# Layer 3's expert MLP in a 13-stage graph network: tokens as the stationary operand, slots on the partitions

## What is computed

```
router_probs = softmax(xf @ router_w);  expert_index = argmax;  expert_gate = max
position_in_expert = cumsum(mask) * mask;  mask *= position < C
expert_inputs  = einsum("td,tec->ecd", xf, dispatch)              # (8, 64, 768)
h              = gelu(einsum("ecd,edm->ecm", expert_inputs, w1) + b1)   # (8, 64, 192)
expert_outputs = gelu(einsum("ecm,emd->ecd", h, w2) + b2)         # (8, 64, 768)
out            = einsum("ecd,tec->td", expert_outputs, combine);  x = x + out
```

## Time and profile before

| | |
|---|---|
| median of 3 runs | 3299.75 us (3291.88, 3299.75, 3300.95) |
| the profiled execution | 3296.41 us, span of its instructions 3294.6 us |
| PE busy | 3065.6 us, 93% |
| DVE, ACT, POOL busy | 52%, 23%, 43% |
| the chain that ended last | PE 85%, DVE 9%, issue 3%, ACT 2% |

### The profile page before, as it was taken

The page is one execution under the profiler, slowest core; times in us unless marked ns, Lnnn a source line. Parts: engine busy times, 40 slices in busy tenths (PEclk is TensorE's granted clock), DMA queues, the critical chain, the costliest instruction groups (busy, mean ns, idle before and its releaser), DMA issues.

```text
span 3294.6 us, 38724 instructions
## 1 busy us (share of the span) xinstructions
PE 3065.6 (93%) x13979; PEld 2397.6 (73%) x13979; DVE 1713.4 (52%) x2808; ACT 754.8 (23%) x1333; POOL 1427.1 (43%) x1007
## 2 busy tenths in 40 slices
PE   8999899999999987898997989899999998989978
PEld 3577577888888884676776468578888886778858
DVE  7734699474556435636765546433344436641141
ACT  1043211232333212102244122211111103121222
POOL 2022287524544360563440045366666664536600
PEclk9999899899999998998998999999999999999987
DMA  2011266212222121222210232133333322213313
GB/s 82 15 48 44 91 192 222 70 43 68 75 72 66 58 82 40 87 86 64 66 58 10 71 112 72 45 93 99 96 95 95 95 86 67 72 48 100 96 32 132
DMA packets 92132, 259.35 MB, mean 79 GB/s; under 512 B 10431, under 2 KB 11071, under 8 KB 91716
## 3 DMA queue, kind: packets, MB, share of 16 engines
q1 hardware_dynamic: 80352, 219.45, 21.8%
q10 hardware_dynamic: 11652, 38.19, 3.5%
HBM read 256.03 MB, written 1.57 MB: 78 GB/s over the span
## 4 chain that ended last, share of the span: by engine, by line
PE 85%; DVE 9%; issue 3%; ACT 2%; DMA 0%; ACTq 0%; DVEq 0%
PE ps L429 22%; PE ps L433 22%; PE ps L434 22%; DVE aux L2004 3%; PE ps L909 2%; PE ps L537 1%; PE ps L531 1%; PE ps L1269 1%; PE ps L995 1%; PE ps L801 1%; PE ps L790 1%; PE ps L783 1%; PE ps L775 1%; DVE hot L2454 1%; DVE row L1814 1%
## 5 line engine op out<-in xcount | busy, mean ns | idle before, releaser
L367 POOL TENSOR_SCALAR w_hi<-raw 128x768 fp32r<-128x768 f32 x498 | 461.9, 928 | 1654.6 <-PE ps L429 1445.6
L370 POOL TENSOR_TENSOR w_lo<-raw,w_hi 128x768 fp32r<-128x768 f32 x498 | 973.6, 1955 | 41.5
L429 PE MATMUL ps<-H_hi,w_hi 128*128 128x512 f32 x804 | 319.9, 398 | 21.1 <-issue 11.6
L429 PE MATMUL ps<-A_hi,w_hi 128*128 128x512 f32 x780 | 309.2, 396 | 12.1 <-ACT scr L1594 12.1
L433 PE MATMUL ps<-H_lo,w_hi 128*128 128x512 f32 x804 | 316.6, 394 | 0.0
L434 PE MATMUL ps<-H_hi,w_lo 128*128 128x512 f32 x804 | 316.5, 394 | 0.0
L429 PE MATMUL ps<-B_hi,w_hi 128*128 128x512 f32 x720 | 292.2, 406 | 21.3 <-DVE B_lo L1798 15.2
L433 PE MATMUL ps<-A_lo,w_hi 128*128 128x512 f32 x780 | 305.7, 392 | 0.0
L434 PE MATMUL ps<-A_hi,w_lo 128*128 128x512 f32 x780 | 305.2, 391 | 0.0
L433 PE MATMUL ps<-B_lo,w_hi 128*128 128x512 f32 x720 | 283.3, 393 | 0.0
L434 PE MATMUL ps<-B_hi,w_lo 128*128 128x512 f32 x720 | 283.1, 393 | 0.0
(11 more groups left out here) (490 smaller groups left out, 5802.1 us busy)
## 6 DMA issues: line engine op xcount, KB each, us to landing
raw<-stream_dram SPq DMA_DIRECT2D x558, 384.0 KB, 3.1
w_ring<-w_dram ACTq DMA_DIRECT2D x45, 384.0 KB, 3.6
u_rows<-rows_dram ACTq DMA_DIRECT2D x8, 768.0 KB, 5.8
rows<-rows_dram ACTq DMA_DIRECT2D x7, 768.0 KB, 4.0
w_last<-w_dram ACTq DMA_DIRECT2D x9, 384.0 KB, 3.6
x<-x_dram ACTq DMA_DIRECT2D x1, 1536.0 KB, 9.4
out_dram<-x ACTq DMA_DIRECT2D x1, 1536.0 KB, 5.1
orf<-orf_dram ACTq DMA_DIRECT2D x6, 192.0 KB, 3.0
```

The costliest lines, as they stand in the source:

```text
L367: pool.tensor_scalar(w_hi[:, b // 3, b % 3], raw[:, b // 3, b % 3], 1.0, 1.0, ALU.mult, ALU.mult)\
L370: pool.tensor_tensor(w_lo[:, b // 3, b % 3], raw[:, b // 3, b % 3], w_hi[:, b // 3, b % 3], ALU.subtract)\
L429: mm = pe.matmul(o, wh, xh, start=first, stop=False, skip_group_check=True)
```

## The change

Only ffn3 and its data change. In step 1 DVE makes all four comparisons without a wait between, then all four casts, each with a signal of its own (PE waits for them tile by tile in the first bank), then the bias selector `row` (8 x 512) and the four scalings. The up product is turned round: 64 slots of one expert are stationary, the 192 unpadded hidden columns move; experts 2m and 2m+1 write to partitions 0 to 63 and 64 to 127 of bank m. DVE copies the bank to scr, PE turns it by two transposes of 128x96 (`slots_turned`), ACT adds b1 and makes the gelu as before on 96 partitions. The down product has 64 slots (96 rows of hidden) stationary and w2's rows move, 384 columns at a time; b2 comes by a matmul of 8 rows in front of each bank. ACT makes the gelu in PSUM and the high part, DVE the low part; the results lie with slots on the partitions, so `to_nodes(scr)` and the split after it go. The transposes of the scaled one-hots move between the down tiles (`weights_turned`, banks 6 and 7). The stream holds 28 used blocks and 2 of zeros in place of 36; ACT issues one more small DMA (slot_b, 8 x 768) behind that of tri. b2 leaves the column table (48 columns fewer in the first load).

```diff
-TURNS = dict(..., mlp3=8, ffn3=6)
+TURNS = dict(..., mlp3=8, ffn3=5)
...
+                            if j == 0 and h == 0:
+                                pe.wait_ge(dve_to_pe, S.due(dve_to_pe))
                             mm = pe.matmul(ps[:, j], bn[:, m, j * P:j * P + P], e_hi[:, m], ...
...
-                for n in range(3):
-                    for f in range(KC):
...
-                                mm = pe.matmul(ps[:, f, c], raw[:, f // 3, f % 3, k], acc[:, k, c], start=k == 0,
...
-                                mm = pe.matmul(ps[:, f, e * 64:e * 64 + 64], raw[:, f // 3, f % 3, k],
-                                               hidden[:, q // 8, q % 8 * 64:q % 8 * 64 + 64], start=h == 0, stop=h == 1,
...
-                to_nodes(scr)
+                def slots_up(m):
+                    use(m)
+                    for c in range(3):
+                        i = 3 * m + c
+                        whole_block(turn + i // 6, i % 6)
+                        for q in range(4):
+                            e, k = (4 * c + q) // KC, (4 * c + q) % KC
+                            if m == 0 and e == 0:
+                                pe.wait_ge(act_to_pe, S.due(act_to_pe))
+                            mm = pe.matmul(ps[64 * e:64 * e + 64, m, 0:FF], acc[:, k, m * P + 64 * e:m * P + 64 * e + 64],
+                                           raw_at(i % 6)[:, q * FF:q * FF + FF], start=k == 0, stop=k == KC - 1,
...
+                        whole_block_used()
+                    done(mm, m, "dve")
+
+                def slots_turned(m):
+                    b = 4 + m % 2
+                    use(m)
+                    use(b)
+                    for h in range(2):
+                        mm = pe.transpose(ps[0:96, b, h * P:h * P + P], scr[:, m, h * 96:h * 96 + 96], ident[:, :])
...
+                    done(mm, b, "act")
+
+                def slots_down(m):
+                    banks = ((0, 1), (2, 3), (4, 5), (0, 1))[m]
+                    pe.wait_ge(act_to_pe, S.due(act_to_pe))
+                    for g in range(2):
+                        use(banks[g])
+                        mm = pe.matmul(ps[:, banks[g], 0:384], row[0:8, m * P:m * P + P],
+                                       w1_ring[0:8, 0, g * 384:g * 384 + 384], start=True, stop=False, skip_group_check=True)
...
+                    for q in range(4):
+                        e, h = q // 2, q % 2
...
+                        for g in range(2):
+                            mm = pe.matmul(ps[64 * e:64 * e + 64, banks[g], 0:384],
+                                           hidden[0:96, m, h * P + 64 * e:h * P + 64 * e + 64],
+                                           raw_at(i % 6)[0:96, g * 384:g * 384 + 384], start=False, stop=h == 1,
...
+                slots_up(0)
+                for m in range(1, NT):
+                    slots_up(m)
+                    slots_turned(m - 1)
+                pe.wait_ge(dve_to_pe, S.due(dve_to_pe))
+                slots_down(0)
+                slots_turned(NT - 1)
+                for m in range(1, NT):
+                    if m < 3:
+                        weights_turned(2 * m - 2)
+                        weights_turned(2 * m - 1)
+                    slots_down(m)
+                for b in range(4, 6):
+                    whole_block(turn + 4, b)
+                unpend()
                 graph_t("dve")
...
+                def slots_out(m):      # ACT
+                    banks = ((0, 1), (2, 3), (4, 5), (0, 1))[m]
+                    for g in range(2):
                         act.wait_ge(tile_for["act"], S.due(tile_for["act"]))
+                        S.step(act.activation(ps[:, banks[g], 0:384], ps[:, banks[g], 0:384], ACT.Gelu_apprx_tanh))
+                        act.copy(bn[:, m, 384 * g:384 * g + 384], ps[:, banks[g], 0:384]).then_inc(act_to_dve, 1)
...
-                    S.step(dve.tensor_copy(e_hi[:, m], aux[:, m]))
+                    dve.tensor_copy(e_hi[:, m], aux[:, m]).then_inc(dve_to_pe, 1)
+                S.step(dve.tensor_copy(row[0:8, :].rearrange("p (e c) -> p e c", e=8), ...
+                for m in range(NT):
                     S.step(dve.tensor_scalar(aux[:, m], aux[:, m], nv[:, 12, m:m + 1], None, ALU.mult))
                 mark(dve_to_pe)
```

More of the change, by code:

```diff
@@ L409, in whole_block, with raw_at @@
                 pe.wait_ge(raw_in[b], turn * 16 + 16)
+            def raw_at(b):
+                return raw[:, b // 3, b % 3].rearrange("p k c -> p (k c)")
             raw_owed = [0]
@@ L1751, in _, with slots_gelu @@
                     mark(act_to_pe)
-                for q in range(16):
+                def slots_gelu(m):
+                    b = 4 + m % 2
                     act.wait_ge(tile_for["act"], S.due(tile_for["act"]))
-                    c, c0 = slice(q % 8 * 64, q % 8 * 64 + 64), 64 * (q // 2)
-                    freed(act.activation(hidden[:, q // 8, c], ps[:, q % 6, c0:c0 + 64], ACT.Gelu_apprx_tanh,
-                                         bias=col("L3_ffn_b1", q)), q % 6)
-                mark(act_to_pe)
@@ L1758, in _ @@
-                for n in range(3):
-                    for f in range(KC):
-                        act.wait_ge(tile_for["act"], S.due(tile_for["act"]))
-                        for e in range(3 * n, min(3 * n + 3, 8)):
-                            c = slice(e * 64, e * 64 + 64)
-                            ins = act.activation(scr[:, f, c], ps[:, f, c], ACT.Gelu_apprx_tanh, bias=col("L3_ffn_b2", e * KC + f))
-                        freed(ins, f)
-                mark(act_to_pe)
-                for m in range(NT):
-                    act.wait_ge(tile_for["act"], S.due(tile_for["act"]))
-                    act.copy(e_hi[:, m], ps[:, m]).then_inc(act_to_dve, 1)
@@ L1769, in _ @@
-                nodes_high()
+                    for e in range(2):
+                        for h in range(2):
+                            c = slice(h * P + 64 * e, h * P + 64 * e + 64)
+                            ins = act.activation(hidden[0:96, m, c], ps[0:96, b, c], ACT.Gelu_apprx_tanh,
+                                                 bias=col("L3_ffn_b1", 4 * m + 2 * e + h)[0:96])
+                    freed(ins, b)
+                    mark(act_to_pe)
+                def slots_out(m):
+                    banks = ((0, 1), (2, 3), (4, 5), (0, 1))[m]
+                    for g in range(2):
+                        act.wait_ge(tile_for["act"], S.due(tile_for["act"]))
+                        S.step(act.activation(ps[:, banks[g], 0:384], ps[:, banks[g], 0:384], ACT.Gelu_apprx_tanh))
+                        act.copy(bn[:, m, 384 * g:384 * g + 384], ps[:, banks[g], 0:384]).then_inc(act_to_dve, 1)
@@ new lines, in weights_high @@
+                def weights_high(m):
+                    act.wait_ge(tile_for["act"], S.due(tile_for["act"]))
+                    act.copy(e_hi[:, m], ps[:, 6 + m % 2]).then_inc(act_to_dve, 1)
+                for m in range(NT - 1):
+                    slots_gelu(m)
+                slots_out(0)
+                slots_gelu(NT - 1)
+                for m in range(1, NT):
+                    if m < 3:
+                        weights_high(2 * m - 2)
+                        weights_high(2 * m - 1)
+                    slots_out(m)
@@ L2780, in kvq, with blocks_of @@
         thirds(w[:, D:2 * D], w[:, 2 * D:], w[:, 0:D])
+    def blocks_of(bs):
+        for n in range(0, len(bs), 3):
+            out.append(np.stack(bs[n:n + 3]).reshape(3, P, KC, P).transpose(2, 1, 0, 3).reshape(D, 384))
     def mlp(w1, w2):
```

104 lines of the change are left out of this document (52 added, 52 removed), and 2 rows, old and new, of the table COLUMNS.

## The result

The kernel after takes 3257.95 us (median of 3256.68, 3257.88, 3258.02, 3262.86) against 3295.82 for the kernel before in the same measurement. The ratio is 0.9896 [0.9867, 0.9925]. In another measurement the same two kernels gave 0.9909 [0.9874, 0.9945], with 3262.3 for after. To read such numbers one must know that the kernel before itself has runs near 3280 and runs near 3298 (in one measurement 5 of 19 from 3279 to 3284 and 14 from 3296 to 3303), and that its profiled execution, 3296.41, is of the second kind.

The account below looks back on a forecast made before the run. The prediction took PE, 85% of the chain, as the bound. Gains of 23.0 us between dispatch and combine and 3.6 before it, together 26.6, gave 3269.8 profiled and a 3273.1 median; it forecast 3271, range 3263 to 3284.

Parts of the forecast that it names:

- Part 1, DVE's order: Before the dispatch: it needs only the comparisons and one cast, so it starts 3.6 us earlier and stays 13.3 us long.
- Part 2, up: Up product: 96 listed matmuls of 192 columns at 0.160 us, 15.4 us instead of 22.6, weight loads hidden.
- Part 3, down: Down product: 80 listed matmuls of 384 columns take 25.6 us at clock 1.00, biases 5.1 of it, instead of 38.8.
- Part 4: Transposes and operand shape changes on PE: 24 transposes cost 2.7 us, 16 shape changes 2.4 us.
- Part 5: Before the combine: PE waits 2.3 us for ACT and DVE to finish the last down tile, instead of 3.0.
- The sum: From the dispatch's end to the combine: 71.4 us becomes 48.4; with part 1 the gain is 26.6, profiled execution 3269.8.
- two halves at once: Rival, up and down: one pass of each half overlaps at every expert border, 2.1 us in all, giving 3269; chance 0.18.
- DMA starves PE: Rival, up and down: weight blocks arrive too slowly at 200 GB/s, +3.4 us, giving 3274; chance 0.06.
- Loads show: Rival: weight loads of 64-wide operands are not hidden, 9 us in all, giving 3280; chance 0.07.
- The clock falls in down: Rival, down: PE's clock drops as it did before in this place, +25.6 us, giving 3297, no change; chance 0.08.
- The clock never rises: Rival: PE stays at 1.2 GHz from dispatch to combine, 53 us more than forecast, giving 3324; chance 0.04.

Follow-up runs that it names:

- one half: Kernel after, but both experts of a bank write to partitions 0 to 63 in up and down, leaving out half the results: 3270.46 us, ratio to before 0.9926.
- row and tail: Kernel after with b2 as row 96 of w2 blocks, no bias matmuls, last down tile in banks 6 and 7, combine begun early: 3253.24 us, ratio to before 0.9862.
- after with a stop: Kernel after, but PE turns the last up tile and waits for all of ACT's gelu before down: 3266.82 us, ratio to before 0.9917.
- before with filling: Kernel before, plus one f32 matmul of 512 columns into unused bank 7 behind each of 18 groups of down products: 3295.63 us, ratio 1.0002.
- before without the stop: Kernel before, but ACT marks the up gelus in three parts so PE need not stop 1.0 us before down: 3295.91 us, ratio 0.9984.

## Why the prediction was right in kind and too small in size

The step that failed is that PE's matmuls were all added up in line, in up and in down, with the overlap of the two halves left at 0 (and at no more than 2.1 us as a rival). The runs show 7.9 us of overlap. The sum for the profiled execution was 3269.8; it came out at 3257.88, 11.9 less. Part by part:

- **Part 1, DVE's order: right.** PE's stop shrank by 3.9 us (said 3.6). The clock did not move against it: the dispatch took 13.55 us against 13.3. The 4.1 us that lie before it belong to no step: 3.1 of them did not come again in the second profile, and the rest is within what the fourteen profiles differ by.
- **Part 2, up: the term that failed, with part 3's.** Said 96 x 0.160 = 15.4; in *one half*, where every matmul waits its turn, it is 16.0 (7.95 + 4.05 + 4.04), so the price of a matmul was nearly right and at most 0.6 us of its weight loads shows. In after it is 13.06 (6.16 + 3.45 + 3.45). The sum had them all in line.
- **Part 3, down.** The 64 listed matmuls, 20.5 by the sum, are 21.2 in *one half* and 16.3 in after. The clock was 1.00 as said. The biases with their changes of shape are 4 x 1.48 = 5.9, said as 5.1 and a part of the shapes' 2.4.
- **Part 4.** Two transposes cost 0.35 and eight about 1.0 with their changes of shape, together 3.4; with the biases' excess of 0.8 that is 4.2 against 2.7 + 2.4 = 5.1.
- **Part 5.** PE stopped for 2.1, said 2.3.
- **The sum.** By the prediction's own reasons the stretch is 48.4; *one half* has 48.64. That it is so close is in part luck, as the matmuls and biases were 2.1 us dearer in line (0.6 in up, 0.7 in down, 0.8 for the biases) and the changes of shape with the transposes 1.7 us cheaper, and the wait 0.2. So is the agreement of the times (3271 said, 3270.46 measured), since that one holds what lies ahead of the stretch and some 1.7 us of low clock in its combine. Nearly all of the error in the stretch is the overlap: 48.64 - 40.74 = 7.9. The rest of the 11.9 is the 4.1 ahead of the changed code.

So the rival *two halves at once* was what happened, and its price was the mis-sized term. It took one pass beside one pass at each border, 5 x 0.16 + 4 x 0.32 = 2.1, as if the first matmul of the new half could start no earlier than the last of the old. The runs show 3.7 or 3.8 passes at each, 7.9, as the new half starts beside the ninth of twelve or the fifth of eight. With 7.9 the sum is 3261.9, and the second profiled execution of after has 3261.02; the first, 3257.88, is lower by luck. The low end of the range, 3263, had used the 2.1. No row bounded that term, so its low end ought to have been the full overlap that the halves allow, not one pass that I had pictured.

The Trainium skill (TensorE: Matmul & The Clock Gate, Part 3) says that matmuls on different tiles run concurrently and still start and end in program order. The first holds in these traces: 48 matmuls take 4.05 us when alternated. Of the second only the end is borne out, by the order of the signals (3195.425, then 3195.468); the recorded starts of the two halves interleave, with the new one four matmuls ahead. Here the measurement decides, and the prediction's one pass per border is what the order of the starts would have allowed.

**The other rivals.** *DMA starves PE* did not occur in after, though PE used blocks faster than reckoned; it occurs as soon as the halves alternate (5.3 us of waits), and in *row and tail* a late block already shortens the overlap. *Loads show* is out: *one half* leaves 0.6 us for it in up and 0.7 in down (21.2 against 20.5), of the 9 feared. *The clock falls in down* did not occur in after, and *after with a stop* shows that it can, for about one tile. Its price as I had it, +25.6 with the clock low to the end of down, was too high: 3.8 us with the stop itself. *The clock never rises* did not occur.

**Where the gain of the change came from.** The stretch lost 30.7 us. By *before with filling*, 18.3 are the clock that the old down lost (17.2 by the pace of up); the other 12.4 are shorter stops behind the dispatch (1.0 + 3.0 became 2.1, so 1.9) and less work, the overlap's 7.9 among it. Part 1 gives 3.9 more, the run of the profile 4.1. That before's lower runs are those in which its down keeps the high clock fits the size, as the means of the two groups in the measurement of 19 runs lie 17.1 us apart. But none of the lower runs was traced: it is inferred. Against the lower runs of before (mean 3281.6) after (mean 3262.4 in the same measurement) gains 19 us, against the upper ones 36. What decides, in a run of before, whether the clock falls stays open: taking the stop away did not settle it, as waits for blocks took its place.

## What to carry to other kernels

If products on half the array's columns must be done one after the other, order them so that the halves alternate, or at least meet often: each meeting hid 3.7 or 3.8 listed matmuls here, and full alternation halved the time, as long as the blocks of weights were there. A stage whose pace is set by 128-wide f32 weight loads for 64 moving columns is at risk twice: it is slow at 1.00, and in the four traces in which the clock fell in it, it stayed low to the end of the stage. Making the narrow operand the stationary one helped; wide matmuls in between kept the clock but cost as much as they gave. Before judging a total of a few us, compare the stretch that was changed, since the part ahead of it moved by 3.1 us between two profiles of the same kernel and by 6.6 over all fourteen.

## What the runs showed of the hardware that I had not expected

- Matmuls that lie in different columns of the array overlap by 3.7 to 3.8 listed matmuls where the program goes from one expert to the next, at 0.16 us a matmul as at 0.32; alternated, 48 matmuls of 192 columns take 4.05 us against 7.95.
- By the recorded starts the new half begins four matmuls ahead of its turn (3193.247, ahead of 3193.403, 3193.565 and 3193.728 of the old half), while the signals keep the program's order (3195.425, then 3195.468).
- With PE 100% busy on 64-column f32 matmuls the mean granted clock was 0.53 over 31.7 us, though the same matmuls ran at 1.00 through the 21.6 us of up; with 512-column ones in between (36 listed among 192) the same stage ran at 1.00 for 37.1 us, and a stage of 384-column ones was back at 1.00 before 16 of them had ended.
- A wait need not be long for a fall to follow: in *before without the stop* the only ones between the dispatch and the fall were 0.31 and 0.54 us. That they caused it isn't shown.
- Few rows save nothing: f32 matmuls with 8 rows and 384 columns start 0.32 us apart like those with 96 rows, and with the changes of shape around them four take 1.48 us, 0.37 each. A bias is cheaper as one more row of a product (5.1 us less for 16 listed matmuls).
- The stream gave the core 305 GB/s over 19 us at a DMA share of 0.90 (*row and tail*), with no listed wait of PE in them.
